# Row sums of the cross attention: from GpSimd's adds to TensorE's ones products

## What is computed

```python
x = x + attention(layernorm(x))            # 16 heads of 32, softmax over all 512 keys
x = x + cross_attention(layernorm(x), ctx) # queries from x, keys and values from ctx, causal
x = x + ffn(layernorm(x))                  # 512 -> 2048, gelu, -> 512
```

```python
scores = einsum('bhqd,bhkd->bhqk', qh, kh) / sqrt(32)
scores = where(tril(ones(sq, sk)), scores, -inf)
attn = softmax(scores, axis=-1)      # exp(s - max) / sum of the exps
out = einsum('bhqk,bhkd->bhqd', attn, vh)
```

## Time and profile before

| | us |
|---|---|
| median of 3 runs | 1224.34 |
| lowest, highest run | 1221.7, 1225.97 |
| the profiled execution's own time | 1223.58 |
| its span in the trace | 1221.8 |

### The profile page before, as it was taken

One profiled execution on the slowest core, in us unless ns is written; L12 is line 12 of the kernel. 1 busy time (PEld: TensorE's weight loads), 2 busy tenths in 40 slices (PEclk: granted clock), 3 DMA queues, 4 the chain that ended last, 5 costly groups with the idle time before them and its releaser, 6 DMA issues.

```text
span 1221.8 us, 15866 instructions
## 1 busy us (share of the span) xinstructions
PE 1162.2 (95%) x6016; PEld 774.1 (63%) x6016; DVE 674.4 (55%) x966; ACT 483.3 (40%) x792; POOL 431.5 (35%) x398
## 2 busy tenths in 40 slices
PE   5989999999999899999999999999999999999998
PEld 4645566466556544555656565655787887887886
DVE  5656757665776467567667567564454233233222
ACT  4345544545453556535445454554131111111110
POOL 1226632643444756534426347564101001001000
PEclk9979999999999999999999999999999999999999
DMA  6823322342143434514525436420320000000000
GB/s 234 265 87 116 110 77 74 107 122 86 55 119 104 138 109 125 151 62 141 164 86 150 118 104 190 122 69 1 95 87 1 35 1 1 34 0 0 35 1 35
DMA packets 73735, 110.30 MB, mean 90 GB/s; under 512 B 6976, under 2 KB 45888, under 8 KB 71744
## 3 DMA queue, kind: packets, MB, share of 16 engines
q1 hardware_dynamic: 70864, 102.00, 27.8%
q0 software_dynamic: 2080, 6.82, 2.0%
q10 hardware_dynamic: 720, 0.54, 0.1%
HBM read 71.58 MB, written 37.75 MB: 89 GB/s over the span
## 4 chain that ended last, share of the span: by engine, by line
PE 83%; DVE 8%; POOL 3%; ACT 3%; issue 2%; DMA 1%; SPq 0%; DVEq 0%; ACTq 0%; POOLq 0%
PE PS L865 17%; PE PS L866 16%; PE PS L867 16%; PE PS L997 12%; PE PS L982 9%; PE PS L960 8%; DVE m_cols L1203 5%; PE PS L992 2%; PE PS L985 1%; PE PS L963 1%; DVE xTL L1169 1%; ACT PT L784 1%; POOL P_sum L648 1%; POOL P_sum L654 1%; PE PS L879 1%
## 5 line engine op out<-in xcount | busy, mean ns | idle before, releaser
L1203 DVE TENSOR_REDUCE m_cols<-PS 128x1 f32<-128x512 f32 (+3 forms) x432 | 281.8, 668 | 170.2 <-PE PS L960 96.8
L784 ACT ACTIVATE PT<-PS 128x512 f32<-128x512 f32 (+1 forms) x432 | 240.4, 580 | 158.0 <-PE PS L982 69.0
L648 POOL TENSOR_TENSOR P_sum<-PT 128x512 f32<-128x512 f32 x128 | 161.4, 1281 | 355.0 <-ACT PT L784 354.9
L960 PE MATMUL PS<-stackK,stackQ 96*128 96x512 f32 (+3 forms) x512 | 188.3, 404 | 12.2 <-DVE m_cols L1203 10.3
L982 PE MATMUL PS<-stackQ,stackK 100*128 100x512 f32 (+3 forms) x512 | 181.9, 399 | 6.7 <-ACT PT L784 6.5
L837 ACT ACTIVATE hid<-PS,b1c 128x512 f32<-128x512 f32 x64 | 44.1, 690 | 280.2 <-PE PS L867 278.2
L1284 DVE CAST hidH<-hid 128x512 fp32r<-128x512 f32 x64 | 30.6, 478 | 225.0 <-ACT hid L837 222.9
L960 PEld LDWEIGHTS PS<-stackK,stackQ 96*128 96x128 f32 x512 | 92.4, 192 | 80.8 <-DVE m_cols L1203 45.0
L1211 DVE RECIPROCAL P_sum<-PS 128x512 f32<-128x512 f32 x32 | 107.5, 3358 | 56.3 <-PE PS L997 56.3
L982 PEld LDWEIGHTS PS<-stackQ,stackK 100*128 100x128 f32 x512 | 90.3, 190 | 67.5 <-ACT PT L784 30.3
L654 POOL TENSOR_TENSOR P_sum<-P_sum,PT 128x512 f32<-128x512 f32 x96 | 120.5, 1282 | 4.5
(11 more groups left out here) (112 smaller groups left out, 1685.9 us busy)
## 6 DMA issues: line engine op xcount, KB each, us to landing
scratch<-stage SPq DMA_DIRECT2D x128, 256.0 KB, 2.9
stackK<-scratch SPq DMA_DIRECT2D x62, 256.0 KB, 3.9
stackQ<-scratch SPq DMA_DIRECT2D x46, 256.0 KB, 3.7
stackQ<-scratch SPq DMA_DIRECT2D x18, 512.0 KB, 4.8
stackK<-scratch SPq DMA_DIRECT2D x60, 128.0 KB, 4.1
stackQ<-scratch SPq DMA_DIRECT2D x28, 128.0 KB, 3.6
PT<-wT SPq DMA_DIRECT2D x3, 1024.0 KB, 8.6
x_res<-x SPq DMA_DIRECT2D x3, 1024.0 KB, 9.1
```

The source lines that it names most:

```text
L648: pool.tensor_tensor(P_sum[:, h, :], PT[:, h, :], PT[:, 4 + h, :], ALU.add).then_inc(p_added, 1)
L784: nc.scalar.activation(PT[:, slot:slot + heads, q0:SEQ], PS[:, T_BANK + n % 2, 0:heads * width].rearrange("p (h n) -> p h n", h=heads), AC ...
L960: mm = nc.tensor.matmul(dst[:, a, :], stackQ[0:STACK, par, h + a, q * P:(q + 1) * P], stackK[0:STACK, par, h + a, 0:n], start=a == 0, stop ...
L1203: nc.vector.tensor_reduce(m_cols[:, q, STACK + h:STACK + h + heads], PS[:, S_BANK + m % 2, 0:heads * n].rearrange("p (h n) -> p h n", h=he ...
```

## The change

In the cross layer, `weigh_values` issues a second group of four products behind that of the values: the same tile of `PT`, at the same width, with the block of ones in the place of the values, into `R_BANK`. `p_used` is counted up behind it, for all four key tiles. `sum_rows` does nothing in the cross layer. GpSimd adds nothing there, its memset of a part of `PT` at the first cross unit is gone, and so are ScalarE's waits for its adds. In the self layer nothing changes.

```diff
 def adds_before(u):
-    cross = max(u - FIRST_CROSS, 0)
-    return (u - cross) * 2 * HPG + cross * (HPG + HPG // ADD_HEADS[CROSS])
+    return min(u, FIRST_CROSS) * 2 * HPG
...
             for u in range(UNITS):
                 b, g = divmod(u, GROUPS)
-                if u == FIRST_CROSS:
-
-                    pool.wait_ge(p_used, FIRST_CROSS * KT)
-                    pool.memset(PT[:, 4:8, 0:P], 0.0).then_inc(zeroed, 1)
-                    pool.wait_ge(zeroed, 1)
                 for n in raws_of(u, 0.0, 3.0):
                     low_raw(n)
                 for h in range(HPG):
                     if u and h == 2:
                         low_output(u - 1)
-                    add_probabilities(u, 1, h)
+                    if layer_of(u) == SELF:
+                        add_probabilities(u, 1, h)
                 for n in raws_of(u, 3.0, 9.0):
                     low_raw(n)
-                for h in range(0, HPG, ADD_HEADS[layer_of(u)]):
-                    add_probabilities(u, 2, h)
+                if layer_of(u) == SELF:
+                    for h in range(HPG):
+                        add_probabilities(u, 2, h)
...
                     act.wait_ge(p_used, KT * u + 3)
-                    act.wait_ge(p_added, adds_until(u, 2, 1))
+                    if layer_of(u) == SELF:
+                        act.wait_ge(p_added, adds_until(u, 2, 1))
...
-                if k == 2:
-                    act.wait_ge(p_added, adds_until(u, 1, h + heads - 1))
-                elif k == 0 and u:
-                    act.wait_ge(p_added, adds_until(u - 1, 2, h + heads - 1))
+                if k == 2 and layer_of(u) == SELF:
+                    act.wait_ge(p_added, adds_until(u, 1, h))
+                elif k == 0 and 0 < u <= FIRST_CROSS:
+                    act.wait_ge(p_added, adds_until(u - 1, 2, h))
...
                 mm = four_heads(O_BANK, q0, lambda h: V[:, k, (g * HPG + h) * HEAD:(g * HPG + h + 1) * HEAD],
                                 lambda h: PT[:, (4 * k + h) % 8, q0:SEQ], k == 0, k == KT - 1)
-                if k < KT - 1:
+                if layer_of(u) == CROSS:
+
+                    mm = four_heads(R_BANK, q0, lambda h: ones[:, :], lambda h: PT[:, (4 * k + h) % 8, q0:SEQ],
+                                    k == 0, k == KT - 1)
+                if k < KT - 1 or layer_of(u) == CROSS:
                     mm.then_inc(p_used, 1)
 
             def sum_rows(u):
-                q0 = queries(u, KT - 1)
+                if layer_of(u) == CROSS:
+                    return
                 pe.wait_ge(p_added, adds_before(u + 1))
                 four_heads(R_BANK, 0, lambda h: ones[:, :], lambda h: P_sum[:, h, :], True, False)
-                four_heads(R_BANK, q0, lambda h: ones[:, :], lambda h: PT[:, 4 + h, q0:SEQ],
-                           False, True).then_inc(p_used, 1)
+                four_heads(R_BANK, 0, lambda h: ones[:, :], lambda h: PT[:, 4 + h, :], False, True).then_inc(p_used, 1)
```

More of the change, by code:

```diff
@@ L96, in stacked @@
     return 2 * DMA * sum(len(stack_loads(a)[late]) for a in range(u % 2, u + 1, 2))
-ADD_HEADS = {SELF: 1, CROSS: 2}
 def adds_before(u):
-    cross = max(u - FIRST_CROSS, 0)
-    return (u - cross) * 2 * HPG + cross * (HPG + HPG // ADD_HEADS[CROSS])
+    return min(u, FIRST_CROSS) * 2 * HPG
 def adds_until(u, k, h):
-    return adds_before(u) + (h + 1 if k == 1 else HPG + h // ADD_HEADS[layer_of(u)] + 1)
+    return adds_before(u) + (k - 1) * HPG + h + 1
 GENERAL = [6, 7]
@@ L413, in decoder_layer @@
         p_added = sem("p_added")
-        zeroed = sem("zeroed")
         r_done = sem("r_done")
@@ L641, in add_probabilities @@
             def add_probabilities(u, k, h):
-                heads = ADD_HEADS[layer_of(u)] if k == 2 else 1
-                pool.wait_ge(p_ready, fills_until(u, k, h + heads - 1))
+                pool.wait_ge(p_ready, fills_until(u, k, h))
                 if k == 1:
@@ L651, in add_probabilities @@
                         pool.wait_ge(p_added, adds_until(u, 1, HPG - 1))
-                    q0 = queries(u, k)
-                    sums = P_sum[:, h:h + heads, q0:SEQ]
-                    pool.tensor_tensor(sums, sums, PT[:, h:h + heads, q0:SEQ], ALU.add).then_inc(p_added, 1)
+                    sums = P_sum[:, h, :]
+                    pool.tensor_tensor(sums, sums, PT[:, h, :], ALU.add).then_inc(p_added, 1)
             root(0)
```

## The result

The changed kernel takes 1262.34 us (median of 3 runs, 1260.58 to 1269.16) against 1224.34: 1.032 times the time of before, 95% interval 1.027 to 1.038. I had forecast 1255.5 with a range up to 1261. Direction and most of the size were right, and about 7 us were missing from the sum.

The account below looks back on a forecast made before the run. TensorE, busy 95% of the span, was taken to bound the kernel. 34.1 - 1.07 - 1.3 - 0.25 = 31.5 us on the profiled 1223.58 gave 1255.1, forecast as 1255.5, with an 8 in 10 range of 1249 to 1261.

Parts of the forecast that it names:

- The price of the ones products: Behind the cross units' value groups: 64 added groups, 2.13 us a unit, 34.1 us over 16 units, nothing for loads.
- The sums' removal gives nothing at 15 turns: At turns between cross units: sums of 1.22 us end together with ScalarE's copy of the maxima, so removal gains 0.
- Unit 31's gain of 1.07 us: Last cross unit, which has no turn: removing the sums' 640 columns directly behind the last values saves 1.07 us.
- The waits that take in an added group: In g = 0 units and units 29 and 30, existing waits absorb 0.21 us each, 1.3 us back in all.
- GpSimd's adds give up 0.25 us: Unit 28: TensorE waited 0.56 for a late norm against 0.31 in unit 20; ending the adds saves 0.25 us.
- The last addition: Final sum: 31.5 us added to the profiled execution gives 1255.1; the runs' median is 0.8 higher; forecast 1255.5.
- The step that failed: Behind the turns: without the sums TensorE idles 1.2 us and starts scores at the same distance; priced at zero.
- The range: 8 in 10 range for the whole kernel, 1249 to 1261, including part of a payback and half the loads' cost.
- all cases and rivals: Own case 1252 to 1258, 81%; sums' time back 7%; waits absorb ones 5%; loads show 5%; faster 1%; ones free 1%.

Follow-up runs that it names:

- experiment 5: The changed kernel with the ones group of key tile 0 issued twice in each cross unit: 1277.44 us, 1.0443 of before.
- a filler: The changed kernel with an added, never-read ones group, 512 columns wide, behind turns between cross units: 1256.33 us at all 15, 1256.71 at the last three.
- experiment 6: The changed kernel with GpSimd's adds and ScalarE's waits for them kept, their result unused: 1265.27 us.
- the one with all fillers: The changed kernel with one more, never-read ones group behind each of the 15 turns between cross units: 1256.33 us, 1.028 of before.
- experiment 7: The changed kernel again, 1260.47 us; with one added ones group behind the turn into unit 30 alone, 1263.18, or into unit 31 alone, 1264.03.
- experiment 3: The kernel before without the P_sum products in the cross layer, GpSimd's adds kept: 1231.7 us, 1.0066 of before.
- that with three: The changed kernel with one more, never-read ones group behind the last three turns only, into units 29, 30 and 31: 1256.71 us, 1.0275 of before.

## Why the prediction was right and wrong

- **The price of the ones products** (34.1 us): right to about 1 us. 0.85 us at 512 columns by experiment 5, and nothing for the loads. But the good sum, 31.75 us measured at full clock against 31.5, is partly luck: a unit with g = 1 got 2.17 us longer (17.54 to 19.71), where 2.13 less the payback of 0.04 is 2.09, so the 64 groups cost about 35 us by an estimate from these two units, and paybacks that were given nothing or too little made up for it.
- **The sums' removal gives nothing at 15 turns**: right in its mechanism. The scores came 1.75 us after the turn in the changed kernel, with a filler, and without the P_sum products alone; the payback was 0.04 us a turn, 0.6 in all. Unit 31's gain of 1.07 us is right too: with the clock up it lasts 19.8 us from its turn to the feed-forward product, against 18.8, so 1.0 more instead of 2.1.
- **The waits that take in an added group**: right. The wait for the transposed rows of unit 20 is 0.43 instead of 0.66, the turn's wait in unit 29 0.45 instead of 0.67.
- **GpSimd's adds give up 0.25 us**: misread, and its cause open. The 0.56 us at 780.06 is not the same place as unit 20's 0.31, which in unit 28 stands one group of transposes later. So the late norm's extra wait was all of the 0.56. After the change it is 0.17, and 0.39 us are won; the kernel before, then the changed one:

```profile
781.25 0.63 PE L879 MATMUL PS<-ident,PT 128*128 128x128 f32 x4 [0.31 <-ACT PT L730]
```

```profile
806.95 0.63 PE L870 MATMUL PS<-ident,PT 128*128 128x128 f32 x4 [0.17 <-ACT PT L721]
```

With the adds kept this extra wait was gone altogether (experiment 6: no wait there, unit 28 0.3 us shorter than in the changed kernel), so that run doesn't show that the adds' end won it. The term is small enough not to matter.
- **The last addition** has a slip: 1255.1 for the profiled execution and 0.8 more for the median is 1255.9, not 1255.5. It decides nothing.
- **The step that failed** is "TensorE stands idle for those 1.2 us and starts the scores at the same distance from the turn", priced at zero. The start is right, the price is not: behind such holes at the last turns TensorE fell to the lower clock. I had read the clock, 1.00 throughout, and kept it as a constant in all cases and rivals, though the change turned 15 times 1.2 us of TensorE's work into idle time, at three places next to idle times of 0.67 and 0.65 us that stood in the earlier trace rows in front of me. This term was 0 and should have been +6.95 us: the cross layer of the changed kernel less that of the one with all fillers, 387.2 - 380.25.
- **The range** was built from costs of instructions alone, so no part of it held this. A rival "the holes of the last units bring the clock down" would have been priced from rows at falls like the one that the trace of before shows in unit 12 (a mean of 0.93 over 25 us, so 3.5 us at half clock and 1.7 us lost), and one at each of the last three turns would have brought the forecast to 1260 to 1261.

The clock follows what TensorE did before, as the table of experiment 7 shows, 14 falls behind 20 open turns and none behind 19 closed ones. This is also what the Trainium skill says ("TensorE: Matmul & The Clock Gate", Part 1), a gate with two levels, set by how busy the engine has been. The trace agrees as to the levels, 0.50 and 1.00.

## What to carry to other kernels

Before you count a removed piece of work on the busiest engine as a gain, look at what ends during it: if the next piece's other input becomes ready only then, the work was free, and removing it leaves a hole. Before you count a hole as free, look for other idle times near it and at the clock: on TensorE a hole can slow the work behind it, and useful or even useless work in it can be worth more than its absence. Work that must be added belongs into such holes first.

## What the hardware showed that I had not expected

- Less work was slower: 14 us of products taken off TensorE made the kernel 0.7% slower (experiment 3), and 2.7 us of useless products at three places made the changed kernel 4 to 6 us faster (1256.7 against medians of 1260.5 and 1262.3).
- Within the cross layer the clock fell only in the last three units, though the same hole of 1.1 us stands at all 15 turns. In twelve units with it the granted clock stayed at 1.00. The difference lies in the idle times beside it (experiment 7).
- The fall isn't the same in every execution of one kernel. The changed kernel's runs go from 1259 to 1269 us with mean granted clocks of 0.989 to 0.978. Part of that has nothing to do with the change: unit 15, a self unit that is the same in both kernels with fillers, took 23.70 us at clock 1.00 in the profile with all of them and 24.85 us at 0.95 in that with three, and all of the 3.3 us between their spans lies ahead of the cross layer. Times of single executions a few us apart tell nothing here until the stretches are compared.
